# A transformer layer with routed experts on one core: projection, routing, scatter and shared rows merged into one stage, weights split during attention

## The reference, cut to what matters

```python
# x: (8, 512, 256), 16 heads of 16, 16 experts of width 128, two chosen, shared expert of width 512
x = x + layernorm(attention(layernorm(x), w_qkv, w_out, b_out))      # rotary embedding, softmax
y = layernorm(x)
shared = (silu(y @ sfc1.T) * (y @ sfc2.T)) @ sfc3.T
logits = y @ gate_w.T
top_w, top_idx = top_k(logits, 2); top_w = softmax(top_w)
dispatch = zeros(T, 16); dispatch[t, top_idx[t]] += top_w[t]
h = silu(einsum('td,ehd->teh', y, w1))
moe = einsum('teh,te,edh->td', h, dispatch, w2)
out = x + layernorm(moe + shared)
```

## Time and profile before

| | |
|---|---|
| median of 3 runs | 1047.65 us (1046.75 to 1048.17) |
| profiled execution, its own time | 1047.89 us |
| its span | 1046.1 us, mean TensorE clock 0.896 |
| PE busy | 828.5 us (79%) |
| DVE busy | 662.2 us (63%) |
| ACT busy | 578.1 us (55%) |
| POOL busy | 382.6 us (37%) |
| DMA | 111.31 MB, mean 106 GB/s |

### The profile page before, as it was taken

How to read it: one execution, slowest core, us unless ns; L and a number is a source line. 1 busy time by engine, 2 the same in 40 slices (tenths; PEclk the granted TensorE clock), 3 DMA queues, 4 the chain that set the end, 5 groups by cost and what they waited for, 6 DMA issues and landing times. The chain is left out here.

```text
span 1046.1 us, 15606 instructions
## 1 busy us (share of the span) xinstructions
PE 828.5 (79%) x4978; PEld 530.1 (51%) x4978; DVE 662.2 (63%) x1172; ACT 578.1 (55%) x1147; POOL 382.6 (37%) x446
## 2 busy tenths in 40 slices
PE   4379999999999999999965677419980999839873
PEld 3245444444444444433325566308870998727662
DVE  4377787787777777787704888673330666506664
ACT  2117767776776767777754766323430677604443
POOL 4350513315060421400002444306674477743342
PEclk9769999999999999999996976658995999959897
DMA  7776647284655827363002212003443466437111
GB/s 135 152 186 119 131 101 165 82 173 92 143 102 112 174 72 123 71 120 45 3 19 59 56 55 56 0 23 114 134 138 123 141 199 188 149 116 224 41 56 61
DMA packets 84717, 111.31 MB, mean 106 GB/s; under 512 B 15134, under 2 KB 56608, under 8 KB 84642
## 3 DMA queue, kind: packets, MB, share of 16 engines
q1 hardware_dynamic: 77730, 93.51, 38.4%
q0 software_dynamic: 6912, 16.86, 4.6%
HBM read 55.62 MB, written 50.48 MB: 101 GB/s over the span
## 5 line engine op out<-in xcount | busy, mean ns | idle before, releaser
L411 DVE TENSOR_REDUCE negmax<-ring 128x2 f32<-128x1024 f32 x256 | 309.3, 1219 | 91.5 <-PE ring L558 89.4
L366 ACT ACTIVATE probs<-score 128x512 f32<-128x512 f32 x512 | 278.7, 599 | 80.7 <-PE score L570 80.7
L570 PE MATMUL score<-q_st,k_st 64*128 64x512 f32 x512 | 210.1, 469 | 11.4 <-ACT probs L366 9.0
L558 PE MATMUL ring<-k_st,q_st 48*128 48x512 f32 x512 | 181.9, 459 | 10.3 <-DMA k_st<-rows_in 7.3
L570 PEld LDWEIGHTS score<-q_st,k_st 64*128 64x128 f32 x512 | 83.7, 185 | 151.4 <-ACT probs L366 99.4
L582 PE MATMUL av<-probs,v_aug 128*32 128x512 f32 x1024 | 136.4, 604 | 2.6 <-ACT probs L366 1.2
L278 POOL CAST part_r<-negmax 128x16 fp32r<-128x16 f32 x32 | 6.3, 196 | 301.3 <-DVE negmax L411 301.3
L1308 POOL DMA_INDIRECT rows_out<-m_y,m_rows x80 | 78.8, 985 | 48.1 <-ACT m_y L1335 31.6
L558 PEld LDWEIGHTS ring<-k_st,q_st 48*128 48x128 f32 x512 | 70.1, 190 | 15.3 <-issue 8.1
L1343 DVE TENSOR_TENSOR m_xlo<-m_bx,m_xhi 128x512 fp32r<-128x512 f32 x40 | 27.7, 691 | 64.3 <-ACT m_xhi L1319 64.3
L152 POOL TENSOR_TENSOR scratch<-qk_raw,cos 128x512 f32<-128x512 f32 x30 | 38.3, 1278 | 60.4 <-ACT qk_raw L317 58.3
(11 more groups left out here) (218 smaller groups left out, 1888.9 us busy)
## 6 DMA issues: line engine op xcount, KB each, us to landing
q_st<-rows_in SPq DMA_DIRECT2D x96, 128.0 KB, 4.2
k_st<-rows_in SPq DMA_DIRECT2D x96, 128.0 KB, 5.7
rows_wide<-pad SPq DMA_DIRECT2D x20, 516.0 KB, 5.5
m_rows<-rows_wide SPq DMA_DIRECT2D x40, 258.0 KB, 3.0
weights<-rows_out SPq DMA_DIRECT2D x16, 512.0 KB, 9.1
X<-in_x SPq DMA_DIRECT2D x8, 512.0 KB, 10.0
rows_in<-turned_hiq SPq DMA_DIRECT2D x16, 256.0 KB, 2.6
rows_in<-turned_loq SPq DMA_DIRECT2D x16, 256.0 KB, 2.5
```

The costliest lines, as they stand in the source:

```text
L366: nc.scalar.activation(probs[r // 2 % 2][r % 2][:, a, :], score[:, a, :], ACT.Exp, scale=HD ** -0.5).then_inc(exp_done, 1)
L411: nc.vector.tensor_reduce(negmax[Gn % 2][:, t, 2 * p:2 * p + 2], ring[t % 2][:, :, :], AX.X, ALU.max, negate=True).then_inc(max_done, 1)
L558: last = nc.tensor.matmul(half[:, a, :], q[rows, t * P:(t + 1) * P], k[rows, :], start=True, stop=True)
L570: nc.tensor.matmul(score[:, a, :], k[rows, kt * P:(kt + 1) * P], q[rows, :], start=True, stop=True).then_inc(sc_ps, 1)
```

## The change

- **Attention.** The fills of `rows_wide` go, but for one small one. In groups 2 to 26 the expert and shared weights, `w_out`, the gate and the bias pass in 24 chunks of 512 columns through one buffer: SP loads a chunk, ACT casts its high part behind round 0 of the next group, GpSimd subtracts, SP stores both parts to `split` in DRAM.
- **One merged stage** (`LAST = B + 1`, ten steps s) in place of the second and third block, written out without register loops: in step s the projection and first norm of row s, the routing of row s-1, the slots of row s-2 and the scatters of rows s-2 and s-3, and two chunks of the shared expert for five rows (0, 2, 4, 6, 7). `weights` is loaded from `split`. Each expert has a region of its own in DRAM, so that a token's slot is expert x region + rank, and the rank comes from a running count per row. The residual add and the powers are on GpSimd, and the exponential of the routing is a power of e.
- **Tiles and last stage in one block.** A pair is loaded by two DMAs at addresses from a table. Behind the 40 pairs the same engines go on with shared rows 1, 3 and 5. The expert outputs of the five early rows are added to `O` by accumulating DMAs from GpSimd, and seven rows are added to the output in the same way.

```diff
@@ attention: SP @@
+        def load_chunk(c):
+            if c > 0:
+                sp.wait_ge(chunk_out, 32 * c)
+            if c < CHUNKS - 2:
+                sp.dma_start(chunk[:, :], experts_t[:, c * N:(c + 1) * N]).then_inc(chunk_in, 16)
...
+        def store_chunk(c):
+            sp.wait_ge(chunk_low, c + 1)
+            for k, src in enumerate((chunk_hi, chunk)):
+                sp.dma_start(split_v[c, k], src[:, :].bitcast(F32).rearrange("p (a r) -> p a r", r=P)).then_inc(chunk_out, 16)
...
-            if 0 <= G < FILLS:
-                sp.dma_start(fill[G], pad[:, :].unsqueeze(1).broadcast_to([P, fill.shape[2], ROW])).then_inc(filled, 16)
+            if chunk_at(G - 1) is not None:
+                store_chunk(chunk_at(G - 1))
+            if chunk_at(G) is not None:
+                load_chunk(chunk_at(G))
@@ attention: GpSimd, before max_split(G + 1) @@
+            if chunk_at(G - 1) is not None:
+                c = chunk_at(G - 1)
+                pool.wait_ge(chunk_high, c + 1)
+                nc.gpsimd.tensor_tensor(chunk[:, :], chunk[:, :], chunk_hi[:, :].bitcast(F32), ALU.subtract).then_inc(chunk_low, 1)
@@ attention: ACT, at the end of a round @@
+            if r == 0 and chunk_at(G - 1) is not None:
+                c = chunk_at(G - 1)
+                act.wait_ge(chunk_in, 16 * (c + 1 + c // (CHUNKS - 1)))
+                nc.scalar.copy(chunk_hi[:, :], chunk[:, :]).then_inc(chunk_high, 1)
@@ merged stage: TensorE @@
+            for s in range(LAST + 1):
+                a, b = 2 * s - 2, 2 * s - 1
+                project(s)
...
+                if s % 2 == 0:
+                    first(a)
+                    second(a - 1)
+                    turn("xt", s - 1)
+                    rank(s - 2)
+                    gate(s - 1)
+                    turn("ot", s + 1)
+                    first(b)
+                    logits(s - 1)
+                else:
+                    second(a - 1)
+                    turn("xt", s - 1)
+                    turn("ot", s + 1)
+                    rank(s - 2)
+                    gate(s - 1)
...
+                    first(a)
+                    logits(s - 1)
+                    first(b)
+                if s > 0:
+                    second(a)
@@ merged stage: GpSimd @@
+            for s in range(LAST + 1):
+                scatter(s - 3, 1, 0)
+                if live(s):
+                    first_scale(s)
+                scatter(s - 3, 1, 1)
+                if live(s):
+                    add_rows(s)
+                scatter(s - 2, 0, 0)
+                if live(s) or live(s - 1):
+                    powers(s)
+                scatter(s - 2, 0, 1)
@@ merged stage: ACT @@
+            def keep(i):
+                b = ROWS[i]
+                act.wait_ge(y_s, i * SC + SC)
+                for h in range(2):
+                    act.wait_ge(first_rows[h], 32 * (b + 1))
+                    act.wait_ge(copied[h], 32 * (b + 1))
...
@@ tiles: SP @@
-                sp.dma_start(rows[s % LOADS][:, :, :], in_v[s]).then_inc(loaded[s % LOADS], 16)
+                for f in range(2):
+                    at = sp.snap(at_r[(2 * s + f) % AT], min_val=0, max_val=RECORDS - P)
+                    sp.dma_start(rows[s % LOADS][:, f, :], rows_in[bass.ds(at, P), :]).then_inc(loaded[s % LOADS], 16)
@@ tiles and last stage: GpSimd, behind the 80 scatters @@
+            def add(j, k):
+                if k == 1:
+                    pool.wait_ge(sent[j], sends(j) + 16)
+                pool.dma_start(tiles(O, ROWS[j]), moe_v[k, ROWS[j]], accum_op=ALU.add).then_inc(sent[j], 16)
...
+            all_sent(pool)
+            add(0, 0)
+            for j in range(EARLY):
+                if j + 1 < EARLY:
+                    add(j + 1, 0)
+                add(j, 1)
+            pool.wait_ge(x_out, 16 * (B - 1))
+            for j in range(B):
+                row_scale(j)
+                if EARLY + j // 2 < B and j % 2 == 0:
+                    pair_sum(EARLY + j // 2)
+                if j > 0:
+                    add_to_output(j - 1)
```

More of the change, by code:

```diff
@@ L20, with attention @@
 AX = mybir.AxisListType
[L23 to L28 removed]
+def attention(nc, ctx, x_in, w_qkv, cos_in, sin_in, ident_in, turns, rows_in, split, later_weights, X, O, ident, pad):
     def sb(name, shape, dt=F32):
@@ L616, in attention @@
     return sync_engine, gpsimd_engine, scalar_engine, vector_engine, tensor_engine
[L619 to L633, removed]
-        self.round, self.n = round_, 0
-    def step(self, instruction):
-        self.n += 1
-        instruction.then_inc(self.semaphore, 1)
-        self.engine.wait_ge(self.semaphore, self.round * self.per + self.n)
-def for_rows(engine, row):
-    row(0)
-    with engine.Fori(1, B) as b:
-        row(b)
 def run_block(nc, sync=None, gpsimd=None, scalar=None, vector=None, tensor=None):
@@ new lines, in feed_forward, with part @@
+    tables_i = sb("tables_i", [2, TILES], I32)
+    split_v = split.rearrange("c p a k r -> p c a k r")
+    def part(T, c0, n):
+        return [T[:, c0 // P:(c0 + n) // P, k, :].rearrange("p a r -> p (a r)") if n == P else
+                T[:, c0 // P:(c0 + n) // P, k, :] for k in range(2)]
+    weight = lambda c0, n: part(weights, c0, n)
+    tr_s, hi_s, lo_s, a_s, g_s, silu_s, h_s, hh_s, hl_s, y_s, kept_s = (
+        sem("shared_" + x) for x in "tr hi lo a g silu h hh hl y kept".split())
@@ L1286, in feed_forward @@
[L1286 to L1291 removed]
+        msem = lambda name: sub.enter_context(nc.semaphore("m_" + name))
@@ L1548, in vector @@
+            for m in range(M0, M1):
+                i, n = m // SC, m % SC
                 multiply(m)
-                if m - 1 in SLOT:
-                    scale_of_mean(SLOT[m - 1])
-                if m in SLOT:
-                    whole(SLOT[m])
+                if m - 1 in NORM_AT:
+                    scale_of_mean(NORM_AT[m - 1])
                 hidden_low(m)
-                if n == SC - 1 and r + 1 < B:
-                    low(r + 1)
-                if m in SLOT:
-                    statistics(SLOT[m])
@@ L1558, in vector @@
-                if m - 2 in SLOT:
-                    residual(SLOT[m - 2])
-            whole(B - 1)
+                if n == SC - 1 and i + 1 < B:
+                    low(i + 1)
+                if m in NORM_AT:
+                    statistics(NORM_AT[m])
+            scale_of_mean(B - 2)
             statistics(B - 1)
-            residual(B - 2)
             scale_of_mean(B - 1)
-            residual(B - 1)
+            dve.wait_ge(z_s, B * QT)
+            nc.vector.tensor_tensor(tiles(X, ROWS[-1]), tiles(X, ROWS[-1]), tiles(O, ROWS[-1]), ALU.add).then_inc(whole_s, 1)
@@ L1603, in feed_forward @@
+            for i in range(EARLY, B):
+                pe.wait_ge(lo_s, (i - EARLY + 1) * DC)
+                first(i * SC)
+                for n in range(1, SC):
+                    first(i * SC + n)
+                    if n == SC - 1 and i + 1 < B:
+                        transposes(i + 1)
+                    second(i * SC + n - 1)
+                second(i * SC + SC - 1)
         run_block(nc, sync=sync, gpsimd=gpsimd, scalar=scalar, vector=vector, tensor=tensor)
```

1551 lines of the change are left out of this document (804 added, 747 removed).

## The result

The changed kernel takes 1109.45 us (median of 4 runs, 1103.96 to 1112.37) against 1047.91 us beside it: a ratio of 1.057, 95% interval 1.051 to 1.063. The forecast was slower by 7 us, with a range up to 1100; it was slower by 61. The profiled execution took 1108.34 us, its span 1106.5. Medians leave out executions over 1.5% above the fastest of their kernel, which changes those of `mid_cast` (two left out), `mid_keep` (one) and `plain_loads` (one, of 3118.5 us). In a later set of runs, that of `late_load`, `load_keep_early` and `fewer_rows`, the kernel before itself took 1102 us. Nothing recorded says why; attention is not longer there, while a tile loop with nine buffers takes 139 to 140 us from first to last scatter, where the same loop takes 110 to 115 in the other sets. Numbers of that set are compared within it alone, and two of its kernels were run again.

A forecast was written before the change was run, and what follows sets the result against it. The prediction took TensorE to bound attention (to 545.4 us) but not the 500.7 us behind it. It summed 1047.9 +104 (attention) -52 (merged stage) -45 (tiles and last stage) = 1055 us, range 980 to 1100.

The forecast's parts named there:

- Then the tenth is issued at +148.5: Last block: GpSimd issues the tenth accumulating DMA 148.5 us after the block's start; the block's term was -45 us.
- The term (+104, bounds 77 to 140): Attention: 88 us of waits for chunks plus 16 us of TensorE at a lower clock.
- Turns 0 and 2: Attention: ACT waits for a chunk 10.9 us six times and 4.6 us five times, 88 us together.
- I take 0 of a bound of 1: Attention, turns 1 and 3: the 6 us trip ends about when ACT is ready, so no wait is charged.
- the walk: Merged stage: even and odd step followed through four engine orders, TensorE 18.5 and 18.8 us; 20.5 us a step taken.
- The term missed by 12 us: Merged stage: 208 us in place of 260.5, -52 us, bounds -70 and -31.
- Delays the casts behind it by some 4 us: Merged stage, odd steps: ACT's `keep` first waits for the scatter just issued, delaying later casts some 4 us.
- the 19 us: Merged stage: GpSimd's add can hold DVE once a step, up to 19 us; none taken, 19 kept for the upper bound.
- GpSimd's 80 scatters stay at 1.29 us and bound the tiles: Tiles: scatters set the pace, the last ending 121.5 us after the start.
- 2 us to issue and 6 to land: Last block: cost taken for each accumulating DMA; bounds 1 and 4 us, or 4.5 and 9 us.
- The prediction's own sign of being wrong: Last block: the prediction is wrong if the accumulating adds take much more than 25 us together.
- rival 3: Merged steps held by GpSimd's lock and late casts (-31+19), slow accumulating DMAs (-20), with +104: 1120 us; chance 0.12.

The follow-up runs named there:

- mid_cast: chunk_first with ScalarE's cast in round 4 and GpSimd's subtraction right behind `max_split`: 1056.40 us, ratio 1.008 to the kernel before.
- mid_keep: Changed kernel with the edits of mid_cast and late_keep together: 1039.34 us, ratio 0.991 to the kernel before.
- plain_loads: Changed kernel with sixteen plain loads by SyncE, summed on GpSimd and VectorE, in place of accumulating transfers from `rows_out`: 1101.82 us, ratio 1.051.
- late_load: Changed kernel with each chunk's load, cast (round 7), subtraction and stores in one group: 1035.45 us, ratio 0.941; run again (late_load_again) 1003.67 us, 0.957.
- load_keep_early: Changed kernel with late_load, late_keep and early_scale together: 1017.82 us, ratio 0.925; run again 974.55 us, ratio 0.931.
- fewer_rows: Changed kernel with seven buffers for the tiles' rows in place of nine: 1183.41 us, ratio 1.074, in the set of late_load.
- chunk_first: Changed kernel with SyncE's chunk stores and next load ahead of the turn's last placements, cast still in round 0: 1025.28 us, ratio 0.976.
- late_keep: Changed kernel with ScalarE's `keep` behind the logits in odd merged steps, no longer first: 1090.66 us, ratio 1.037.
- before_eight: Kernel before the change with eight buffers for the tiles' rows in place of ten: 1077.48 us, ratio 1.030.
- early_scale: Changed kernel with `row_scale(0)` to `(2)` between the accumulating transfers, not behind the tenth: 1097.02 us, ratio 1.047.
- late_cast: Changed kernel with the chunk's cast in round 6 in place of 0 and GpSimd's subtraction last in its group: 1018.58 us, ratio 0.969.

## Why the prediction was right in kind and wrong in size

The direction and attention's waits were forecast rightly. What failed is the size: +7 us was forecast and +61 measured, because three terms were mis-sized in one direction, attention by 18 us, the merged stage by 12 and the last block by 23. The last block failed most, in the step "Then the tenth is issued at +148.5"; it was at +168.5.

- **The attention stage**: right in mechanism and place. chunk_first and late_load_again show it: the same chunks, casts and stores in another order give back 80 and 96 us of the stage. The term (+104, bounds 77 to 140) measured +122. Turns 0 and 2 cost 89.5 us against 88 (in the working, turn 2's lateness is 249.7 less 244.55, so 5.1 and not 5.2). The misses are "I take 0 of a bound of 1" for turns 1 and 3, where turn 1 and the first chunk cost 11.3, and the rest, put down to the clock, which came to 22 and not 16. One trip of turn 1 is in the trace: second store at 340.38, load issued at 343.29, cast at 345.97. That is 5.6 us, less than the 6 taken, and it ended 0.85 us after ACT was ready, within the bound of 1; the other five ended 1.5 to 2.8 us after, which is outside it. The Trainium skill, "DMA: Bandwidth & Descriptors", section "Anatomy of one DMA — SWDGE (gpsimd) path", gives 2.6 us for one 256 KB transfer, as an estimate from its rule for GpSimd's path; SyncE's last store (2.9) and load (2.7) come near it.
- **The merged stage**: the walk was right in its order, 17.6 us for an even step and `keep` waiting in the odd ones. The term missed by 12 us, 8 of them in the full steps. "Delays the casts behind it by some 4 us" fits step 3 (late_keep took 4.0 us off it) and is too small for step 5 (6.4 us), and so is the 20.5 us a step made of it. In step 5 TensorE stood 4.2 us and then ran 512-column matmuls at 0.63 us in place of 0.40, at a clock of 0.61; in late_keep it stood 1.0 us there and ran at 1.00. I had charged a fall of the clock behind each wait of turn 0 in attention, and none here. In the whole stage the wait cost 19.8 us.
- **VectorE held beside GpSimd's add**: it happens (one 128x8 instruction of VectorE took 2.19 us beside the add of 2.18 us at 763.0, where its kind takes 0.17). What it costs the stage was not measured, so whether none of the 19 us was the right charge stays open.
- **Tiles**: "GpSimd's 80 scatters stay at 1.29 us and bound the tiles" was wrong by 9 us: each issue stays at 1.29 us, but the last scatter ends at +130.4 and not +121.5. The change takes one of ten row buffers, which I did not count. fewer_rows and before_eight show that two buffers fewer lengthen the loop by 32 us and more; for the step from ten to nine this is an inference.
- **Accumulating transfers**: "2 us to issue and 6 to land" measured 1.29 and 9.6, and the tenth was issued 20 us late. The tiles end 9 us late, the first transfer starts 8 us late, and the ten take 36 us in place of 24. That second transfers wait for first ones was in those 24 (ten issues of 2 are 20); the landing that this chain goes through was too short. In the same chain 1.29 and 9.6 make about 33 us, an estimate. The prediction's own sign of being wrong, adds that take much more than 25 us together, thus came true. The wait at the first `scale_of_mean` was foreseen (10 us, measured 13.9), and early_scale gives back 9 us of the part by moving the powers alone. (In the working, +139, 10 us held and six times 5.6 make +182.6 and not +180.6.) By the same section of the Trainium skill's "DMA: Bandwidth & Descriptors", 512 KB would land in 3.2 us, an estimate; here it takes 9.6, and 14.2 with more in flight, so the measurement decides.
- **The range** ended at 1100 because I let in only half of rival 3 and none of attention's upper side with it. Rival 3 had the slow adds right (-20, measured -22) and its merged stage too dear (-12, measured -40), with attention at its middle. The three misses shared a direction, because in each stage I priced the wait that I saw and left what follows it (the next trip, the clock, the landing that the next transfer waits for, the ring one buffer shorter) at nothing or too small.

## What to carry to other kernels

A side job that passes through DMA round trips must be placed in every in-order queue that it touches: put each of its waits behind the work that others need, and leave time between the load and the cast. late_cast and mid_cast each freed one queue and stopped another; late_load, in which no cast waits over 3 us and the scores wait 11 us in all, was worth 103 us. When a change takes memory, count the buffers of each ring before and after: eight in place of ten cost 32 us here.

## What the hardware showed that was not expected

In the last part, transfers of GpSimd's queue took the DMA engines twice as long for each byte as SyncE's. From 1019.5 to 1065 us in the profile after (queue, packets, MB, share of 16 engines):

```profile
q0 software_dynamic: 5280, 5.24, 73.0%
q1 hardware_dynamic: 3168, 3.15, 22.9%
```

That is 0.73x16x45.5/5.24 = 101 engine us (time of one engine, summed over the 16) a MB for the accumulating ones and 53 for the plain ones. Whether the adding or the queue makes the difference was not told apart.
